# Moving the second half's block maxima and scaling of the last feed-forward layer by one and two quarters in a macaron transformer block

## The reference

```python
x = x + 0.5 * ffn(layernorm(x), w_gate, w_up, w_down)      # x: (16, 512, 128)
x = x + attn(layernorm(x), w_q, w_k, w_v, w_proj, ...)     # 16 heads of 64, softmax, layernorm of its result
x = x + 0.5 * ffn(layernorm(x), w_gate, w_up, w_down)      # the last layer

def fp4_quant_dequant(x):                 # along the last dimension, blocks of 16
    scale = max(abs(block)) / 6
    return nearest of {0, .5, 1, 1.5, 2, 3, 4, 6} to abs(block / scale), signed, times scale

def ffn(x, w_gate, w_up, w_down):         # all three products on quantized operands
    h = silu(q(x) @ q(w_gate).T) * (q(x) @ q(w_up).T)      # h: 352 wide
    return q(h) @ q(w_down).T
```

## Time and profile before

| | |
|---|---|
| median of 3 runs | 2203.17 us (2203.1 to 2203.94) |
| the profiled execution's own time | 2205.3 us |
| its span, first to last instruction | 2203.5 us |
| PE busy | 2099.7 us, 95% |
| DVE busy | 1627.1 us, 74% |
| POOL busy | 1429.2 us, 65% |
| ACT busy | 1161.3 us, 53% |

### The profile page before, as it was taken

How to read it: one execution, slowest core, us unless ns; L and a number is a source line. 1 busy time by engine, 2 the same in 40 slices (tenths; PEclk the granted TensorE clock), 3 DMA queues, 4 the chain that set the end, 5 groups by cost and what they waited for, 6 DMA issues and landing times.

```text
span 2203.5 us, 39642 instructions
## 1 busy us (share of the span) xinstructions
PE 2099.7 (95%) x15051; PEld 1164.6 (53%) x15051; DVE 1627.1 (74%) x2633; ACT 1161.3 (53%) x1766; POOL 1429.2 (65%) x1287
## 2 busy tenths in 40 slices
PE   3899999999999999999999999999999999999984
PEld 2455555555555555555555555565555555555543
DVE  5575778778687877878777787877868787776645
ACT  2455555646546555555556555564655646465432
POOL 3375676757577675766767576675757767585643
PEclk8899999999999999999999999999999999999996
DMA  2000000000000000000000000000000000000000
GB/s 61 1 7 2 7 2 2 7 7 7 7 7 7 3 7 7 7 7 2 12 2 7 7 7 7 2 7 7 7 7 6 7 2 7 7 3 7 2 7 10
DMA packets 165786, 15.89 MB, mean 7 GB/s; under 512 B 146592, under 2 KB 165216, under 8 KB 165600
## 3 DMA queue, kind: packets, MB, share of 16 engines
q1 hardware_dynamic: 165600, 13.36, 5.2%
HBM read 7.03 MB, written 4.19 MB: 5 GB/s over the span
## 4 chain that ended last, share of the span: by engine, by line
PE 85%; DVE 9%; issue 3%; POOL 1%; ACT 1%; DMA 0%; SPq 0%; POOLq 0%
PE pS L1042 23%; PE pO L1070 19%; PE pX L1054 6%; PE pX L1094 5%; PE pM L1199 5%; PE pO L1026 5%; PE pM L1026 4%; PE pM L1082 3%; DVE nmax L871 3%; PE FpF L379 2%; PE LpF L379 2%; PE FpF L342 2%; PE LpF L355 2%; PE LpF L342 2%; PE FpF L355 1%
## 5 line engine op out<-in xcount | busy, mean ns | idle before, releaser
L739 POOL TENSOR_TENSOR ES<-ES,E 128x512 f32<-128x512 f32 x512 | 676.7, 1343 | 284.1 <-ACT E L818 280.0
L818 ACT ACTIVATE E<-pS 128x1024 f32<-128x1024 f32 x512 | 524.4, 1024 | 512.8 <-PE pS L1042 505.3
L871 DVE TENSOR_REDUCE nmax<-pX 128x2 fp32r<-128x1024 f32 x512 | 621.8, 1214 | 189.6 <-PE pX L1054 185.8
L1070 PE MATMUL pO<-E,VA 128*64 128x512 f32 x2048 | 524.1, 611 | 2.0 <-DVE KL L989 1.8
L733 POOL TENSOR_TENSOR ES<-E 128x512 f32<-128x512 f32 x256 | 323.0, 1283 | 174.9 <-ACT E L818 174.9
L1054 PE MATMUL pX<-KH,QH 64*128 64x512 f32 x1024 | 248.2, 425 | 11.4 <-DVE nmax L871 8.0
L1042 PE MATMUL pS<-QH,KH 64*128 64x512 f32 x1024 | 255.3, 495 | 0.5 <-ACT E L818 0.5
L1042 PEld LDWEIGHTS pS<-QH,KH 64*128 64x128 f32 x1024 | 95.4, 183 | 235.6 <-issue 230.1
L1054 PEld LDWEIGHTS pX<-KH,QH 64*128 64x128 f32 x1024 | 187.2, 306 | 49.4 <-DVE nmax L871 24.1
L1070 PEld LDWEIGHTS pO<-E,VA 128*64 128x64 f32 x2048 | 114.9, 135 | 168.8 <-issue 168.8
L1042 PE MATMUL pS<-SH,onesr 64*128 64x512 f32 x1024 | 203.4, 393 | 0.0
(11 more groups left out here) (241 smaller groups left out, 3684.6 us busy)
## 6 DMA issues: line engine op xcount, KB each, us to landing
RROW<-RC SPq DMA_DIRECT2D x504, 2.0 KB, 2.0
xin<-in_L_attn_x SPq DMA_DIRECT2D x16, 256.0 KB, 2.8
SH<-nmax SPq DMA_DIRECT2D x256, 2.0 KB, 2.0
LC<-LROW SPq DMA_DIRECT2D x252, 2.0 KB, 2.1
out<-X SPq DMA_DIRECT2D x15, 256.0 KB, 2.5
E<-in_L_attn_w_q SPq DMA_DIRECT2D x1, 512.0 KB, 4.3
E<-in_L_attn_w_k SPq DMA_DIRECT2D x1, 512.0 KB, 5.5
wv<-in_L_attn_w_v SPq DMA_DIRECT2D x1, 512.0 KB, 6.6
```

The lines of the kernel that those rows point to most:

```text
L739: ins = g.tensor_tensor(ES[i % 3][:, hd, :], ES[i % 3][:, hd, :], E[s][:, hd, :], ALU.add)
L818: a.activation(E[s][:, :, :], pS[:, :, :], ACT.Exp).then_inc(s_exp, 1)
L871: v.tensor_reduce(nmax[px % 2][:, :, t:t + 1], pX[:, :, :], AX.X, ALU.max, negate=True).then_inc(s_max, 1)
L1070: ins = pe_.matmul(pO[half(hd), :], VA[of][:, kt, j * 128 + 64 * hd:j * 128 + 64 * hd + 64], E[kt][:, hd, :], start=kt == 0, stop=kt == KT ...
```

## The change

For the 14 batches of `LastLayer` the maxima of the second half of h go from quarter 44 to 45, POOL's scaling by the inverses from 45 to 47, and ACT's pass from 46 to 47. Rounding (49) and all later steps stay.

```diff
@@ class LastLayer
-    max_h, divide_h, magic_h, round_h, rescale_h = (35, 44), (36, 45), (36, 46), (38, 49), (40, 50)
+    max_h, divide_h, magic_h, round_h, rescale_h = (35, 45), (36, 47), (36, 47), (38, 49), (40, 50)
```

## The result

The changed kernel takes 2211.82 us (median of 6 runs, 2211.57 to 2214.03) against 2203.44 us (6 runs, 2203.1 to 2205.28) for the kernel before: ratio 1.0041, 95% interval 1.0032 to 1.0051. It is slower by 8.4 us. I had forecast slower by 27.8 us. It lies between the 2209 of the rival "neither held" and the 2216 of "second scaling not held", so the rows of the profile have to tell which of them came true.

What follows compares the result with a forecast made beforehand. PE, busy 95% of the span, was taken as the bound. Ten batches at 2.07 us and three at 2.36 gave 27.8 us, added to 2203.2 for 2231; range 2208 to 2254, likeliest case's own 2225 to 2238.

Steps and rivals of the forecast that it cites:

- neither held: Rival: both scalings of the moved chain pass POOL and the chain takes 1.56 us; 5.7 us slower, 2209; chance 0.07.
- second scaling not held: Rival: L233 slips in behind L232 before POOL's add; 12.8 us over before, 2216; chance 0.20.
- The bound, and the freed projection: PE bounds; at pair 3 its projection starts at 375.06 for 375.60, gaining 0.54 us in ten batches.
- End of L253 and start of the chain: On DVE, L253 ends at 379.73, 0.30 us earlier than before; the chain starts 0.08 us before that end.
- L232 held beside L258: At the new place DVE's scaling L232 comes up at about 380.55 beside POOL's rescaling, held until 381.20.
- L233 then meets the first add, 1.26 us: Behind L232, DVE's second scaling is held by POOL's add; both holds together add 1.7 us to the chain.
- A late tile also loses its overlap ... 0.22 more: PE's late tile would take 0.62 us instead of 0.40, adding 0.22 us a batch in 13 batches.
- POOL and ACT at no cost: POOL's later scaling and ACT's pass, done by 386.0, cost nothing, as the next `E` is wanted at 387.7.
- The clock falls: Rival: PE's new gap of up to 2.4 us lowers the clock in half of 13 batches, adding 22 us: 2253; chance 0.15.

Runs made afterwards that it cites:

- The pads: The changed kernel plus one scratch reciprocal on DVE ahead of the chain, of 44, 72 or 92 elements: ratios 1.0034, 1.0052 and 1.0176 to the kernel before.
- pool47: The kernel before with maxima left at quarter 44, only POOL's scaling and ACT's pass moved to 47: 2203.48 us, ratio 0.9996.
- max45_pool46: The changed kernel with POOL's scaling and ACT's pass one quarter earlier, at 46, maxima still at 45: 2219.17 us, ratio 1.0071 to the kernel before.
- max46: The changed kernel with the maxima one quarter later, at 46, scaling and pass still at 47: 2209.48 us, ratio 1.0025 to the kernel before.
- pad92: The changed kernel with a scratch reciprocal of 128 x 92 on DVE ahead of the chain: 2237.58 us, ratio 1.0176 to the kernel before.
- lscale46: max46 with the last layer's second scaling of the second half on POOL instead of DVE: 2199.89 us, ratio 0.9986 to the kernel before.
- pad72: The changed kernel with a scratch reciprocal of 128 x 72 on DVE ahead of the chain: 2210.39 us, ratio 1.0052 to the kernel before.

## Why the prediction was wrong, step by step

- **The bound, and the freed projection:** right. The 0.65 us of the earlier trace rows are gone in the ten batches that had them, and the exponentials behind come 0.56 us earlier for it, for the 0.54 forecast.
- **End of L253 and start of the chain:** right in kind. L253 ends at 376.91 and the chain starts 0.08 us before. Measured from the projection, L253 ends 376.91 - 372.22 = 4.69 us behind its start; I had 379.73 - 375.06 = 4.67.
- **L232 held beside L258:** right. It took 0.68 us in 13 of 13, for my "held until 381.20", some 0.65 us.
- **"L233 then meets the first add, 1.26 us":** this step failed. L233 took 0.17 us in 13 of 13. In the sum it stood for 1.15 us a batch, 13 x 1.15 = 15.0 us. I carried a count of ten in 13 from the earlier trace rows to another place without asking by what these ten differed from the three. The pads answer it in part. There L232 had a lead before the end of L258 of 0.64, 0.35, 0.17 and 0.05 us (no pad, 44, 72, 92), and L233 was held in 0, 0, 0 and 13 of 13. So behind L258 it is held only if it comes up when the add has started. The first layer's place is another case. By the single add's own end (368.63 + 1.30, where my forecast halved the pair) the lead there is 0.16 us, L233 and the add are due together, and still it was held ten times. What the two places differ by is not shown (below).
- **"A late tile also loses its overlap ... 0.22 more":** mis-sized. The row for the tile does read 0.62 for 0.40 us. But what follows it starts 380.67 - 380.11 = 0.56 us behind it, and in the kernel before 0.55, as the PE timeline there shows beside the tile of the earlier trace rows:

```profile
382.32 0.39 PE L1164 MATMUL pM<-RROW,sel 64*128 64x512 f32 x1
...
382.87 1.08 PE L1070 MATMUL pO<-E,VA 128*64 128x512 f32 x4
```

382.87 - 382.32 = 0.55. There the tile shared its time with the selection matmul, so it never took 0.40. The matmul's 0.38 us now stand ahead of the gap, and that is no extra: they lie within the lateness of the tile, which I had counted in full from 382.32. So the 13 x 0.22 = 2.9 us are a cost that isn't there; it measured 0.01 us a tile.
- **The sum without these two:** 27.8 - 15.0 - 2.9 = 9.9 us. The profile shows 8.3 at pair 3, the runs 8.4. Most of the difference is the four batches that cost 0.35 us where my sum, without the two terms, has 0.70: 4 x 0.35 = 1.4 us. In these the first layer's L233, held before, now passed, which I had not foreseen.
- **POOL and ACT at no cost:** right for the place where they were put (pool47). One quarter earlier they would have cost 7 us (max45_pool46).
- **The rivals.** "Second scaling not held" is what happened, at 8.4 us for its 12.8; most of the difference is the 2.9 for the overlap and the 1.4 of the four batches. The reason I gave for it, that both have queued up and go together, is not enough: in max46 both had queued up too, and L233 was held in 7 of 13. "Neither held" is out, L232 is held in 13 of 13. "The clock falls" did not happen, since the gap was 0.65 us and not about 2. Where the gap was made 1.70 us (pad92), it did, in eight batches of 13. I had priced a fall at 3.4 us, from 6.8 us at half the clock; in pad92 a fall lasted 3.4 us and cost 1.5.

Two things stay open. The first is what decides when L233 and POOL's next instruction are due together. It isn't the lead: in max46 L232 leads by 0.75 to 0.76 us and L233 is held in 7 of 13. The programs differ in one point. Behind L258 POOL waits for two semaphores (`s_exp`, `s_add`) before its add, though both were long there; between the two adds of a quarter it waits for nothing. Over all twelve traces L233, of either layer, passed in 52 of 52 such meetings behind L258, and between two adds it passed in 68 and was held in 80. That the wait makes the difference is a guess; no run separates it from the kind of instruction ahead. The second is the spread of the kernel before, which is put down to its own race only by argument.

## What to carry to other kernels

A count from one place ("ten of 13 are held") is not the chance of the same event at another: first find what the held and the passed differ by, and if the rows don't show it, as here, give both outcomes at the new place a price and a like chance. A chain of small DVE scalings beside a stream of POOL work costs by its holds more than by its length; give the second of them to POOL, and that hold is gone (lscale46, 3.1 us faster than before where max46 was 5.8 slower). And take what a late matmul costs from the start of the next one, not from its own duration.

## What the runs showed of the hardware

**Who gets in between two POOL instructions.** A DVE scaling that comes up while a POOL instruction runs waits for its end (0.68, 0.39 and 0.22 us for leads of 0.64, 0.35 and 0.17). A second scaling, queued right behind it and due together with POOL's add, then gets through ahead of that add in 39 of 39 cases behind L258. It is held for the rest of the add, 1.28 us, in 13 of 13 when it comes up 0.09 us behind the add's start (pad92). Between the two adds of a quarter the same meeting goes either way: held in 10 of 13 batches before, 8 of 13 in the changed kernel and 1 of 13 in pad72, all at leads of 0.15 to 0.17 us, and in 7 of 13 in max46 at 0.75. The Trainium skill, "SBUF — State Buffer", section "Who interferes with whom", has the lock and the block for the whole of an instruction issued before; the traces agree with that, and it leaves open which of the two is issued first when both are due.

**The clock behind a single gap.** In pad92 PE stands idle for 1.70 us ahead of the tile at 383.23, and the granted clock fell a little later. Windows of pad92 (stretch, length, busy of PE, PEld, DVE, ACT and POOL with counts, granted clock, DMA share, GB/s):

```profile
376.00:381.00 5.00, 5.00 (x37) 2.72 (x33) 4.51 (x7) 1.52 (x2) 2.81 (x3) 1.00 0.07 2
381.00:384.90 3.90, 2.20 (x12) 0.71 (x9) 3.73 (x5) 1.74 (x2) 3.90 (x4) 1.00 0.00 0
384.90:388.30 3.40, 3.40 (x15) 2.10 (x17) 2.45 (x13) 1.21 (x3) 2.73 (x3) 0.50 0.00 0
388.30:392.00 3.70, 3.70 (x25) 1.88 (x23) 1.01 (x1) 2.24 (x5) 0.20 (x1) 0.99 0.00 0
```

PE is full again when the clock goes from 2.4 to 1.2 GHz, and in the stretch of 3.4 us it does 15 of the matmul records where the next 3.7 us hold 25. A pair of score matmuls there reads 0.63 us, for 0.39 at full clock:

```profile
380.67 0.39 PE L1045 MATMUL pS<-QH,KL 64*128 64x512 f32 x2
...
386.55 0.63 PE L1045 MATMUL pS<-QH,KL 64*128 64x512 f32 x2
```

A fall like this came in 8 of the 13 batches with such a gap, and in none with the 0.65 us of the changed kernel. So one hold of DVE by POOL, 1.28 us long, is paid twice: as PE's gap and, in eight batches, as 1.5 us of PE's clock.
